# Inverse deviations and softmax reciprocals as powers on GpSimd, and one exponential over two PSUM banks for two of a step's heads

## The reference, cut to what matters

```python
def _layernorm(x, axis=-1, eps=1e-05):
    m = jnp.mean(x, axis=axis, keepdims=True)
    v = jnp.var(x, axis=axis, keepdims=True)
    return (x - m) / jnp.sqrt(v + eps)
...
        scores = jnp.einsum('bhqd,bhkd->bhqk', q, k) * scale
        attn = jax.nn.softmax(scores, axis=-1)
        out = jnp.einsum('bhqk,bhkd->bhqd', attn, v)
...
    x = x + _L0_attn_ref(_layernorm(x, axis=-1), ...)
    x = x + _L0_ffn_ref(_layernorm(x, axis=-1), ...)
```

## Time and profile before

| | us |
|---|---|
| median of 3 runs | 2427.51 (2425.11 to 2431.14) |
| profiled execution, its span | 2427.3 |
| attention (steps up to the last maximum) | 46 to 1471 |
| one full batch (64 steps) | 179.3 |
| busy in the span: PE, DVE, ACT, POOL | 2283.2, 1891.8, 1632.3, 886.1 |

### The profile page before, as it was taken

The page is one execution under the profiler, slowest core; times in us unless marked ns, Lnnn a source line. Parts: engine busy times, 40 slices in busy tenths (PEclk is TensorE's granted clock), DMA queues, the critical chain, the costliest instruction groups (busy, mean ns, idle before and its releaser), DMA issues. The chain is left out here.

```text
span 2427.3 us, 44076 instructions
## 1 busy us (share of the span) xinstructions
PE 2283.2 (94%) x16398; PEld 1340.3 (55%) x16398; DVE 1891.8 (78%) x3506; ACT 1632.3 (67%) x3168; POOL 886.1 (37%) x1223
## 2 busy tenths in 40 slices
PE   5899999999999999999999988899997999999996
PEld 4233334334334334334333323788886888888886
DVE  5999999999999999999999994466654555555553
ACT  2599999999999999999999987323323343333432
POOL 4051451451451451441542220000003666666664
PEclk8799999999999999999999999799998999999998
DMA  2000011010010010010010010332322545454443
GB/s 76 1 18 1 1 36 36 1 50 22 1 55 17 9 61 3 19 53 1 19 36 1 19 36 18 126 100 78 104 61 81 115 109 112 87 112 113 100 99 35
DMA packets 104364, 122.74 MB, mean 51 GB/s; under 512 B 7553, under 2 KB 91393, under 8 KB 104193
## 3 DMA queue, kind: packets, MB, share of 16 engines
q1 hardware_dynamic: 79616, 86.90, 11.2%
q0 software_dynamic: 24576, 33.57, 8.1%
HBM read 78.50 MB, written 41.94 MB: 50 GB/s over the span
## 5 line engine op out<-in xcount | busy, mean ns | idle before, releaser
L474 DVE TENSOR_REDUCE sb_MX<-ring 128x1 f32<-128x512 f32 x2048 | 1284.5, 681 | 82.0 <-PE ring L782 65.4
L606 ACT ACTIVATE sb_PR<-rot 128x512 f32<-128x512 f32 x2048 | 1123.3, 621 | 102.8 <-PE rot L793 92.3
L782 PE MATMUL ring<-sb_KT,sb_QT 32*128 32x512 bf16 x2048 | 517.1, 390 | 48.9 <-DVE sb_MX L474 36.5
L804 PE MATMUL pv<-sb_PR,sb_VA 128*32 128x512 f32 x4096 | 547.0, 606 | 2.9 <-ACT sb_OT L661 0.6
L782 PEld LDWEIGHTS ring<-sb_KT,sb_QT 32*128 32x128 bf16 x2048 | 128.1, 91 | 632.9 <-DVE sb_MX L474 565.8
L793 PE MATMUL rot<-sb_QT,sb_KT 32*128 32x512 bf16 x2048 | 422.1, 386 | 1.6
L1095 ACT ACTIVATE ex_GL<-ex_gu 128x512 f32<-128x512 f32 x128 | 76.4, 597 | 347.4 <-PE ex_gu L63 345.2
L1162 DVE TENSOR_TENSOR ex_HF<-ex_GL,ex_gu 128x512 f32<-128x512 f32 x128 | 87.5, 684 | 250.8 <-ACT ex_GL L1095 250.8
L1059 POOL DMA_INDIRECT out<-ex_YS,ex_rows_out x128 | 208.8, 1631 | 44.3 <-issue 43.8
L1016 POOL TENSOR_TENSOR ex_pool_scratch<-identity 128x1 f32<-128x1 f32 x96 | 35.1, 366 | 477.6 <-POOLq L859 332.0
L61 PE MATMUL ex_gu<-ex_XH,weights_high 128*128 128x512 f32 x512 | 200.4, 391 | 2.4 <-DVE ex_XL L1154 2.4
(11 more groups left out here) (168 smaller groups left out, 4272.2 us busy)
## 6 DMA issues: line engine op xcount, KB each, us to landing
sb_XA<-x SPq DMA_DIRECT2D x8, 1024.0 KB, 5.5
sb_XR<-x SPq DMA_DIRECT2D x8, 1024.0 KB, 5.8
out<-sb_XR SPq DMA_DIRECT2D x8, 1024.0 KB, 4.5
xn<-sb_XN SPq DMA_DIRECT2D x8, 1024.0 KB, 4.5
sh_XG<-xn SPq DMA_DIRECT2D x16, 512.0 KB, 5.5
sh_X<-out SPq DMA_DIRECT2D x16, 512.0 KB, 4.9
weights<-WgT SPq DMA_DIRECT2D x16, 512.0 KB, 4.0
weights<-WuT SPq DMA_DIRECT2D x16, 512.0 KB, 5.6
```

What stands on the lines that cost most here:

```text
L474: nc.vector.reduce_max(MX[:, unit % 2, half, j, qt % 4:qt % 4 + 1], ring[m % RING][:], AX.X).then_inc(ring_done, 1)
L606: out = nc.scalar.activation(PR[V % P_STEPS][:, j, :], R[:], ACT.Exp, scale=0.25)
L782: nc.tensor.matmul(ring[m % RING][:], QT[g][r, P * qt:P * qt + P], KT[g][r, 512 * half:512 * half + 512], start=True, stop=True, tile_posi ...
L804: out = nc.tensor.matmul(pv_bank[head(j), :], VA[b % 2][:, kt, 4 * g + j, :], PR[V % P_STEPS][:, j, :], start=(kt == 0), stop=(kt == TT - 1))
```

## The change

Three things change.

1. The Newton steps go. DVE signals the statistics (`mv_ready`), and POOL computes `rstd` with an addition of eps and a power -0.5 on tiles of 128 by 8 (`inverse_deviation`), at S = 7 for n = 0 and S = 27 for n = 1, and once each at the head and the tail.
2. DVE's reciprocal of the softmax sums goes. POOL computes it in `scale` as a power -1 on a tile of 128 by 16, ahead of its multiplication, and waits for ACT's copy itself.
3. `rot` becomes one tensor of four banks, and in each step two neighbouring heads share one exponential instruction over two banks: heads 0 and 1, or, where head 0 falls on bank 3, heads 2 and 3. ACT counts once for such a pair, when it has ended, and PE waits, for each bank, for the item that last used it.

```diff
+    def place(item, banks=1):
+        at = (AT[-1][0] + AT[-1][1]) % ROT if AT else 0
+        assert at + banks <= ROT
+        ORDER.append(item)
+        AT.append((at, banks))
+        return at
...
+        if V >= 0:
+            at = (AT[-1][0] + AT[-1][1]) % ROT
+            PIECES[V] = ((0,), (1,), (2, 3)) if at == ROT - 1 else ((0, 1), (2,), (3,))
+            for heads in PIECES[V]:
+                place(("ex", V, heads[0]), len(heads))
...
+    EMPTIED, last_in = [], [0] * ROT
+    for n, (at, banks) in enumerate(AT):
+        EMPTIED.append(last_in[at:at + banks])
+        last_in[at:at + banks] = [n + 1] * banks
...
+            def inverse_deviation(n, b):
+                pool.wait_ge(mv_ready[n], b)
+                own.inc(nc.gpsimd.tensor_scalar(var_eps[:], mv[n][:, :, 1], EPS, None, ALU.add))
+                own.wait(pool)
+                nc.gpsimd.tensor_tensor(rstd[n][:], var_eps[:], minus_half[:], ALU.pow).then_inc(rstd_ready[n], 1)
...
-                pool.wait_ge(recip_ready, unit + 1)
+                pool.wait_ge(rot_done, done(("ot", b, unit % UNITS)))
+                own.inc(nc.gpsimd.tensor_tensor(RD[:], AR[:, :, HD], minus_one[:], ALU.pow))
+                own.wait(pool)
...
+                if more and S == 7:
+                    inverse_deviation(0, b + 2)
+                if b and S == 27:
+                    inverse_deviation(1, b)
...
-                if V >= 13 and V % 8 == 5:
-                    weighted((V - 13) // 8)
-                if more and 7 <= S <= 12:
-                    newton(0, 2 * (S - 7))
-                if prev and 26 <= S <= 31:
-                    newton(1, 2 * (S - 26))
...
-                    out = nc.scalar.activation(PR[V % P_STEPS][:, j, :], R[:], ACT.Exp, scale=0.25)
+                    out = nc.scalar.activation(PR[V % P_STEPS][:, j:j + banks, :], rot[:, at:at + banks, :], ACT.Exp, scale=0.25)
...
-                    for j in range(4):
-                        empty(("ex", V, j))
-                        if j == 2 and V >= 9 and V % 8 == 1:
+                    for n, heads in enumerate(PIECES[V]):
+                        empty(("ex", V, heads[0]))
+                        if n == 1 and V >= 9 and V % 8 == 1:
                             evacuate((V - 9) // 8)
...
-            def bank(item):
+            def bank(item, k=0):
                 n = PLACE[item]
-                if n >= ROT:
-                    pe.wait_ge(rot_done, n - ROT + 1)
-                return rot[n % ROT]
+                if EMPTIED[n][k]:
+                    pe.wait_ge(rot_done, EMPTIED[n][k])
+                return rot[:, AT[n][0] + k, :]
...
-                nc.tensor.matmul(R[:], KT[g][r, P * kt:P * kt + P], QT[g][r, 512 * qh:512 * qh + 512], start=True, stop=True,
-                                 tile_position=(r.start, 0)).then_inc(rot_full, 1)
+                out = nc.tensor.matmul(R, KT[g][r, P * kt:P * kt + P], QT[g][r, 512 * qh:512 * qh + 512], start=True, stop=True,
+                                       tile_position=(r.start, 0))
+                if j == heads[-1]:
+                    out.then_inc(rot_full, 1)
```

More of the change, by code:

```diff
@@ L33, in wait @@
         engine.wait_ge(self.sem, self.base + self.n)
[L36 to L53, removed]
 def three(nc, out, hi, lo, stationary, moving, first, last):
@@ L122, in attention @@
             + [("lg", B - 1, half) for half in range(2)])
-    ORDER = HEAD + [item for V in range(-LEAD, LAST)
-                    for item in ([("ex", V, j) for j in range(4)] if V >= 0 else []) + beside(V)] + TAIL
+    ORDER, AT = [], []
+    def place(item, banks=1):
[4 more added lines that the diff above has]
+        return at
+    PIECES = {}
+    for item in HEAD:
+        place(item)
+    for V in range(-LEAD, LAST):
+        if V >= 0:
[3 more added lines that the diff above has]
+                place(("ex", V, heads[0]), len(heads))
+        for item in beside(V):
+            place(item)
+    for item in TAIL:
+        place(item)
     PLACE = {item: n for n, item in enumerate(ORDER)}
     assert len(PLACE) == len(ORDER)
+    EMPTIED, last_in = [], [0] * ROT
+    for n, (at, banks) in enumerate(AT):
+        EMPTIED.append(last_in[at:at + banks])
+        last_in[at:at + banks] = [n + 1] * banks
     def done(item):
@@ L194, in attention @@
         ring = [ctx.enter_context(nc.psum_tensor(f"ring{i}", [P, 512], F32)) for i in range(RING)]
-        rot = [ctx.enter_context(nc.psum_tensor(f"rot{i}", [P, 512], F32)) for i in range(ROT)]
+        rot = ctx.enter_context(nc.psum_tensor("rot", [P, ROT, 512], F32))
         pv_bank = ctx.enter_context(nc.psum_tensor("pv", [P, 512], F32))
@@ L210, in attention @@
         bo_ready = sem("bo_ready")
+        mv_ready = [sem(f"mv_ready{n}") for n in range(2)]
         rstd_ready = [sem(f"rstd_ready{n}") for n in range(2)]
@@ L381, in scale @@
                     ALU.mult).then_inc(ao_ready, 1)
+            inverse_deviation(0, 1)
             pool.wait_ge(ident_in, 16)
@@ L422, in _ @@
             scale(UNITS * B - 1)
+            inverse_deviation(1, B)
         @block.vector
@@ L440, in merge_stats @@
                 for i in tiles:
[L441 to L450, removed]
+                    out = nc.vector.bn_aggr(mv[n][:, i, :], stats[:, i, :])
+                if i == TT - 1:
+                    out.then_inc(mv_ready[n], 1)
             def normalise(n, b, out, src, ready):
@@ L553, in _ @@
                     merge_stats(0, range(4 * (S - 4), 4 * (S - 3)))
-                if more and 7 <= S <= 12:
-                    newton(0, 2 * (S - 7) + 1)
                 if prev and 21 <= S <= 24:
@@ L562, in _ @@
                     merge_stats(1, range(TT))
-                if prev and 26 <= S <= 31:
-                    newton(1, 2 * (S - 26) + 1)
                 if prev and S == 50:
@@ L568, in _ @@
                     finish_gates(b - 1)
-            for unit in range((LAST - 13) // 8 + 1, UNITS * B):
-                weighted(unit)
             for item in TAIL[1:5]:
@@ L583, in _ @@
             merge_stats(1, range(TT))
-            for k in range(RSQRT_STEPS):
-                newton(1, k)
             dve.wait_ge(xn2_out, 16 * (B - 1))
@@ L598, in empty @@
                 n = PLACE[item]
-                R = rot[n % ROT]
+                at, banks = AT[n]
+                R = rot[:, at, :]
                 kind = item[0]
@@ L614, in empty @@
                         act.wait_ge(as_ready, 4 * (b + 1))
-                    out = nc.scalar.copy(XT[:, h, 512 * half:512 * half + 512], R[:])
+                    out = nc.scalar.copy(XT[:, h, 512 * half:512 * half + 512], R)
                 elif kind == "q":
@@ L626, in empty @@
                     _, b, g, n = item
-                    out = nc.scalar.copy((QT, KT)[n][g][:], R[:].bitcast(BF16))
+                    out = nc.scalar.copy((QT, KT)[n][g][:], R.bitcast(BF16))
                 elif kind == "v":
@@ L635, in empty @@
                     qh = n % 2
-                    out = nc.scalar.copy(QT[n // 2][:, 512 * qh:512 * qh + 512], R[:].bitcast(BF16)[:, 0:512])
+                    out = nc.scalar.copy(QT[n // 2][:, 512 * qh:512 * qh + 512], R.bitcast(BF16)[:, 0:512])
                 elif kind == "ot":
@@ L640, in empty @@
                         act.wait_ge(ao_ready, unit)
-                    out = nc.scalar.copy(AR[:], R[:].rearrange("p (a c) -> p a c", c=QUAD)[:, :, 0:HD + 1])
+                    out = nc.scalar.copy(AR[:], R.rearrange("p (a c) -> p a c", c=QUAD)[:, :, 0:HD + 1])
                 elif kind == "bo":
```

25 lines of the change are left out of this document (11 added, 14 removed).

## The result

The changed kernel takes **2453.48 us** (median of 4 runs, 2446.11 to 2454.96) against 2427.12 (4 runs, 2425.11 to 2431.14): ratio 1.0101, 95% interval 1.0084 to 1.0119. It is slower, as forecast, by over twice the 11.5 us of the forecast's sum. The profiled execution has a span of 2453.2 us, 25.9 more than before's 2427.3.

The account below looks back on a forecast made before the run. PE, DVE and ACT lie within 5%; the longest of three loops sets each step. Six full batches +12, batches 0 and 7 +1 each, head and tail -2.5 on 2427.3 gave about 2439 us, range 2405 to 2457.

Parts of the forecast that it names:

- The price of the power: One power on POOL taken as 0.6 us, hidden in the loop, exposed at head and tail.
- The clock: Granted clock of a full batch read as 1.00, the 2.4 GHz level, so left out of the forecast.
- Batches 0 and 7: First and last batch lack half the beside items and one norm each: +1 us each.
- (b): ACT late at pairs on other banks, next item waits for its bank: five a batch, 0.2 to 0.5 each, 1.6 us.
- (a): After steps starting on bank 3, the next head 1 stalls for the pair's bank: 11 x 0.34 = 3.7 us a batch.
- Rival A: Banks don't bind and the change is faster: 2402 us, or 2420 with half of the stalls; chance 0.25.
- rival D: Exponential over two banks slower than a copy of 1024 columns, say 1.15 us: 2453 us; chance 0.05.
- rival B: Stalls and gains cancel, with stalls of 3.3 us a batch: 2425 to 2429 us; chance 0.12.
- Rival C: Power slow on POOL, from about 5 us, delaying biases and ACT's copies of q: 2427 + 12 + 100 us; chance 0.05.
- ACT's saving: Pair's shorter exponential counts where ACT is late, some 20 steps: 20 x 0.045 = 0.9 us a batch gained.
- Newton steps and reciprocals: Removing them from DVE in the loop gains 2.0 us a batch for Newton steps, 0.4 for reciprocals.
- Head and tail: Exposed Newton calls replaced by addition and power: 1.3 us gained at the head, as much at the tail, 2.5 together.

Follow-up runs that it names:

- experiment 2: Kernel before with only the shared exponential over two banks, Newton steps and reciprocals left on DVE: 2458.25 us, ratio 1.0135.
- experiment 4: Changed kernel with each pair's exponential split into two instructions, counted once after the second, so both banks still come back together: 2469.61 us, ratio 1.0162.
- experiment 3: Changed kernel with four single exponentials in steps whose head 0 falls on bank 3, pairs kept in other steps: 2430.55 us, ratio 1.0012.
- experiment 1: Changed kernel with every head's exponential single again, the powers staying on POOL (powers alone): 2412.86 us, ratio 0.9933.
- experiment 6: As experiment 5, with pairs also in light steps and S = 1, 2, 22, 23, where not starting on bank 3: 2409.24 us, ratio 0.9926.
- experiment 8: Kernel of experiment 1 with the reciprocal power in `scale` done twice, holding POOL 5.8 us: 2441.81 us in one run.
- experiment 9: The changed kernel measured once more, unaltered: 2447.08 us, ratio 1.0080.
- experiment 5: Kernel of experiment 1 with pairs in the last twelve steps only and the last two units' reciprocals back on DVE: 2407.07 us, ratio 0.9921.
- experiment 7: Changed kernel with the second logits item moved from S = 48 to 49, swapped with a qT item: 2445.66 us, ratio 1.0077.

## Why the prediction came out as it did

**The steps that failed.** The signs and the mechanism held, the size didn't: 11.5 us by the sum, 25.9 between the spans. Four steps of the prediction failed. The price of the power (0.6) was 1.67 and 2.91, and the last unit's reciprocal, which was not counted, stands on the tail's path: 4.3 us. The clock, set aside, fell in a full batch of this execution: 3.9. Batches 0 and 7, put at half of a full batch's net, cost more: 3.1. And ACT's lateness at a pair (b) was put at five steps a batch and set against a saving of ACT that doesn't show; the overcount in (a) hides most of that: 2.6 over six batches.

**The direction and its mechanism were right.** The sign came from the banks, and the stalls stand where they were put. Plain steps after one on bank 3 take 2.82, with the pair starting 1.81 after head 0 where 1.80 was reckoned, and a stall of 0.33 where 0.32 was. Rival A (the banks don't bind) falls with experiment 2, rival D (the wide exponential is slow) with the 1.04 us and experiment 4, rival B with the time. Rival C, the slow power, falls in the full batches, but at the ends it is what happened: a power over 1.5 us at the head and PE waiting for POOL's `AO`, both named as signs of being wrong, came true (1.67; 3.37 at the tail).
The Trainium skill's "ScalarE: Activation LUTs" (What ACT_TABLE_LOAD costs), from which I had estimated 1.04 for the pair, agrees with the measured 1.038.

**Full batches: +2.0 forecast, +2.4 measured.** Close, but by luck: errors offset each other.
- (a) 3.7 forecast, 2.5 measured (experiment 3). In the trace (against experiment 1) the stalls after bank 3 are 0.30 to 0.43 each, in odd batches after S = 6, 10, 13, 20, 31, 38, 42, 45, 52 and 56. The size of one held; the count did not. An odd batch has 15 steps that start on bank 3 and an even one 17, not 13 or 14; against experiment 3 the step behind stalls in ten and eight of them, 0.2 to 0.4 each, and in odd batches S = 18 and 51 are 0.4 and 0.5 shorter, which gives part of it back.
- (b) less ACT's saving: 1.6 - 0.9 = 0.7 forecast, 2.5 measured (experiment 3 against 1). Step by step between these two traces, the steps named for each kind of batch lose 0.1 to 0.4 each and 1.4 together, close to the forecast; but others (S = 5, 6, 9, 16, 18, 31, 34, 43, 47, 50 and 55, in one kind of batch or both) lose 0.1 to 0.4 too, 1.6 to 1.7 a batch, of which even batches get 0.6 back at S = 51 and 58. The slack of 0.09 that I had found for an item after a pair was too thin to count as cover; that this is the reason in each of them isn't shown.
- ACT's saving by itself doesn't show: what the wide form gains stands in steps that stall (experiment 4), and pairs that don't stall gain nothing (experiment 6).
- Newton steps and reciprocals: 2.4 forecast, 2.6 measured (experiment 1), from the very steps named.

**Batches 0 and 7: +1 each forecast, +2.9 and +2.2 measured.** I halved the net of a full batch. But the net is a difference of two large terms, and they don't halve alike. The pair costs 2.9 in batch 7 (140.2 against 137.4 in powers alone) and 3.2 in batch 0 outside S = 24 and 25, more than half of 5.0. The powers give back only 0.7 in batch 7; in batch 0 they give 0.3 (S = 7 and 12), for the 0.93 of S = 8 isn't there. Each part had to be scaled for itself.

**Head and tail: -2.5 forecast, +1.8 measured.** The failed step is the price of the power. I took 0.6, "nearer to the first by shape"; it is 1.67 for the deviations and 2.91 for the reciprocals. At the head the normalisation starts at 13.30 instead of 13.69: POOL's addition and power replace the Newton calls almost evenly.

```profile
11.25 0.25 POOL L374 TENSOR_SCALAR sb_var_eps<-sb_mv 128x8 f32<-128x8 f32 x1 [2.63 <-DVE sb_mv L465]
11.58 1.69 POOL L376 TENSOR_TENSOR sb_rstd<-sb_var_eps,sb_minus_half 128x8 f32<-128x8 f32 x1
```

At the tail I counted only the deviation. The last unit's reciprocal is on that path too, and went from 0.25 on DVE to 2.90 on POOL; one power more there costs its full length (49.8 in experiment 8 against 46.8 in 1). About 1 of the tail's +2.2 belongs to the execution: experiment 9 has 46.8 where the first profile has 47.9. The bounds (0.23 to 2) held the 1.67 but not the 2.91: an operation that no row shows had been given the range of additions and subtractions.
The Trainium skill's "GPSIMD Engine Reference" (Performance versus the Vector engine), by which I had estimated 0.5, gives its factor of 1.96 for an addition; it doesn't carry over to a power here: 2.91 against DVE's reciprocal of 0.24 is twelve times, and the measurement decides.

**POOL's slack.** That in the loop "the cost is nothing, as long as a power stays under about 5 us", came out right for the full batches, with the wrong bound. At 2.9 the full batches lose nothing; at 5.8 they lose 4, and batch 0 loses at 2.9. I had listed what waits behind `scale` as having "one or more steps in hand", and left out the splits of xt behind S = 21, whose reader is the first projection of S = 24.

**The clock.** That the granted clock of a full batch is 1.00, "so the clock drops out", failed as a step: it was read from before, where no full batch had a drop. In this profile one cost 3.9.

Together: +2.6 in the full batches, +3.1 in the two others, +4.3 at the ends, +3.9 by the drop, +0.6 in the rest: 14.5 more than the sum's 11.5, so 26.0, against 25.9 measured.

## What to carry over

Merging two instructions that empty buffers also merges the return of the buffers: count from when the first of them would have come free to when it is next wanted, before counting what the merge saves (here 0.05 us a step saved, against 5.0 a batch lost in stalls). Give an operation that no row shows a wide range, and look for the one place where it is exposed; work that hides in the loop can be left on the fast engine at the end. And scale gains and losses to partial batches one by one, never their difference.

## What was not expected of the hardware

A power on POOL takes 1.668 us for 128 by 8 and 2.909 for 128 by 16. That is 0.155 us a column and 0.43 beside it, if it goes linearly between and below these two points, which nothing here tests; an addition of 128 by 8 took 0.25.

The granted clock fell to 0.5 inside the loop, for 3.4 to 17.1 us, in two situations. One is when PE had stood idle for POOL's split at S = 24: 1.8 us in batch 0 of experiments 1, 5 and 6, and 3.2 us in batches 1 to 6 of experiment 8, where it repeats in each. It is no rule: experiment 3 has the same 1.8 in batch 0 and no half clock there, nor have before and the changed kernel, with 1.23 and 1.39. The other is around the logits items with their 16-column products (after, experiments 3, 4, 7 and 9), in some batches of an execution and not in others. What tips the second one way or the other stays open. Before and the kernels without pairs that stall (experiments 1, 5, 6 and 8) do the same products and show none in their profiles, and the six at S = 48 all stand in odd batches, where the pair delays S = 47 by 0.2 us. That suggests PE's added waits; but experiment 2 has the pair and shows none, and no run here tests it alone.
